# Quantising the residual stream in steps between the first attention's projection groups, with the last tiles through the score banks and no barrier ahead of the quantised stage

## The chip, the cores and the metric

The kernel runs on the 8 NeuronCores of one Trainium2 chip. Each core works on one sequence of its own (4096 rows of 1024 numbers); the cores share no data, and all run the same program. The metric is the device time in microseconds of the slowest core.

On a core, TensorE (PE) multiplies 128-wide tiles into PSUM, VectorE (DVE) and ScalarE (ACT) work on SBUF and PSUM, GpSimd (POOL) works on SBUF, and SyncE (SP) issues every DMA of this kernel from one queue. Each engine takes its instructions in the order of the program; semaphores connect the engines.

## The reference, cut to what matters

Two layers, each with an attention and a feed-forward part, both of the form `x = x + layernorm(part(layernorm(x)))`:

```python
# attention: 8 heads of 128, causal, no bias
xn  = x / l2norm(x) * sqrt(1024) * gamma
q, k, v = split(xn @ w_qkv.T);  out = softmax(q @ k.T / sqrt(128) + causal) @ v @ w_out.T
# layer 0's second part: product of integers, row scales of both sides
lhs_scale = max(|lhs|, axis=2) / 127          # lhs = layernorm(x)
q_lhs = round(lhs / lhs_scale);  q_rhs = round(rhs / rhs_scale)
acc = q_lhs @ q_rhs;             out = acc * lhs_scale * rhs_scale
# layer 1's second part: three blocks of two 1024 x 1024 linear layers with
# 4-bit weights plus a rank-32 term, a layernorm and gelu between the two
```

What matters here is the seam between layer 0's two parts: every row of `x`, once the attention's output is normalised and added, has to be centred, its absolute maximum taken, scaled and rounded to integers before the integer product.

## The kernel before, in words

The program is written out by hand as one list of steps, `p.add(engine, ...)`; each engine gets its own steps in the order in which they stand there, with waits on semaphores. `PE`, `DV`, `AC`, `GP` and `DMA` add a step to TensorE, VectorE, ScalarE, GpSimd and SP. A DVE step waits for the DVE step before it.

`emit_attn` is one attention. First come the projections to k, q and v for eight blocks of 512 rows (L638, L643). Then 576 *steps* follow, `steps[i] = (qt, h, pr)`: for each block of 512 queries `qt`, each head `h` and each pair `pr` of key tiles of 128 (2 qt + 2 pairs). Step i puts these instructions down, in this order:

- ACT: the exponential of the scores (L765), of which the scores (PE, L756) were put down two steps earlier, into one of two score banks `PS` of 1024 columns; for a pair on the diagonal a mask on POOL (L772).
- PE: the scores of step i+2, then the product of the probabilities with v (L782), and at every second step the row sums (L799) into one bank `RS`.
- At a head's end DVE splits the row sums in a high and a low part (L811, L812); two steps later PE adds the four partial sums (L817, L819) into the bank `MISC`; later ACT forms the reciprocal (L824, L826) and DVE the head's result `feat` (L827).
- When a block of queries is done, its output projection waits in `out_q`: eight *groups*, two halves of 512 columns for each of four row tiles of 128. `out_group` (L850) takes one into `MISC`, every `max(1, (2*qt+2)*H // 11)` steps of the next block. DVE takes statistics of it (L856) and copies it to SBUF (L857). Behind a tile's second half it forms the inverse root in eight column instructions (`rsqrt_eps`, L283 to L288) and updates the residual row tile in one of three buffers (L862), SP stores it to `xbuf` and loads the tile three further into the buffer.
- `quantise_rhs` (a generator) makes the integer weights of the next part, one piece every eight steps.

The last block's eight groups follow after the last step, one after the other through `MISC`. Then comes `p.barrier()`: every engine waits for all that was begun.

`emit_mid` is the quantised stage, on 32 row tiles in pairs, a software pipeline with one pair per turn. `P1` to `P3` load a tile, take statistics (L995), centre it on ACT (L998), take the absolute maximum (L1008), scale (L1021) and round it on ACT (L1023). `Q` transposes the integers on PE and copies them out of PSUM on ACT (L1034); `G` is the integer product (L1043, 32 matmuls a pair). `Y` rescales on DVE (L1051) and sums squares on ACT (L1054); `E1`, `E2` normalise (ACT, L1072) and add to the residual on POOL (L1075); `L1`, `L2` take the next layer's statistics (DVE, L1084 to L1097) and prepare its input (ACT, L1101), `T` transposes that into `xn`. POOL also scales the next layer's weights there, two pieces per turn (`cast_w`, L984).

After a second barrier layer 1's attention runs with the same code, and after a third the last part (`emit_f1`).

## Time and profile before

| | us |
|---|---|
| median of 3 runs | 3982.25 (3980.55 to 4304.46) |
| the profiled execution, its own time | 3971.3 |
| its span, slowest core (core 4) | 3969.8 |
| layer 0: projections | 0 to 477 |
| layer 0: attention steps | 477 to 1321 |
| layer 0: last four tiles' projection | 1321 to 1365 |
| quantised stage, first to last integer product | 1390 to 1703 |
| layer 1: projections | 1728 to 2150 |
| layer 1: attention steps and last tiles | 2160 to 3029 |
| last part | 3040 to 3970 |

Over the span PE is busy for 84%, ACT for 55%, DVE for 53% and POOL for 23%. The profiled execution stands 11 us under the median. The share of the span says little about a stage: PE is busy for 88% of the attention steps and for 55% of the quantised stage. The views used are the windows (busy time of each engine in a stretch), the timeline (instructions with their start, length and the idle time ahead of them) and the groups of instructions by line.

### The profile page before, as it was taken

Reading aid. Unit: us, or ns where it says so; the run is one execution under the profiler, and the core shown is the slowest. Engines: PE = TensorE matmul, PEld = TensorE weight load, DVE = VectorE, ACT = ScalarE, POOL = GpSimd, SP = SyncE. Lnnn points to the kernel's source line nnn. Section 1 sums busy time; section 2 is a strip of 40 time slices with the busy share of each in tenths; the row PEclk is TensorE's granted clock in tenths of the full one; section 3 lists DMA queues with packets and bytes.
Section 4 is the critical chain, followed back from the end, with each engine's and each line's share of the span. In section 5 each row is a group of like instructions: output and inputs, shape, how many; then the busy total and the mean of one; then the engine's idle time right before and its main releaser. Section 6 shows DMA issues by size and latency. Waiting matters only on the chain.

```text
span 3969.8 us, 45734 instructions; the slowest of 8 cores (3946.3 to 3969.8 us)
## 1 busy us (share of the span) xinstructions
PE 3316.4 (84%) x16736; PEld 1382.8 (35%) x16736; DVE 2089.5 (53%) x3897; ACT 2195.0 (55%) x2660; POOL 912.4 (23%) x868
## 2 busy tenths in 40 slices
PE   5999768989999555579997789999994789879997
PEld 2444323333333122233333333333331334334442
DVE  5666455443222488855555544333224656685547
ACT  2211146777888367743332567888891554635543
POOL 2333210001100033236663100000000231433333
PEclk9999879999999777789998899999997899989999
DMA  5111212132110254236655111111003210140004
GB/s 197 53 59 54 97 41 80 64 85 71 52 52 34 80 180 154 85 109 186 181 177 186 43 75 69 54 43 43 22 32 124 101 54 27 38 165 1 1 1 159
DMA packets 93472, 330.47 MB, mean 83 GB/s; under 512 B 12416, under 2 KB 16000, under 8 KB 88384
## 3 DMA queue, kind: packets, MB, share of 16 engines
q1 hardware_dynamic: 93248, 327.56, 24.5%
q8 instruction: 132, 2.16, 0.2%
q14 instruction: 92, 0.75, 0.1%
HBM read 228.94 MB, written 98.57 MB: 83 GB/s over the span
## 4 chain that ended last, share of the span: by engine, by line
PE 55%; DVE 22%; ACT 15%; DMA 3%; issue 2%; POOL 1%; SPq 0%; DVEq 0%; POOLq 0%; ACTq 0%
PE pp L756 9%; PE pp L638 8%; PE pp L782 8%; ACT s_probs L765 6%; PE pp L850 5%; PE pp L643 5%; PE pp L1314 4%; PE pp L1043 4%; PE pp L1269 4%; PE pp L799 3%; ACT f_yg L1301 2%; ACT s_rcp L826 1%; PE pp L622 1%; ACT s_rcp L824 1%; DVE f_r L1293 1%
## 5 line engine op out<-in xcount | busy, mean ns | idle before, releaser
L765 ACT ACTIVATE s_probs<-pp,s_negM 128x1024 bf16<-128x1024 f32 (+2 forms) x1152 | 1123.4, 1039 | 211.1 <-PE pp L756 207.6
L756 PE MATMUL pp<-s_q,s_kT 128*128 128x512 bf16 (+3 forms) x2304 | 664.8, 371 | 74.0 <-ACT s_probs L765 58.5
L782 PE MATMUL pp<-s_probs,s_v 128*128 128x512 bf16 (+3 forms) x2304 | 659.1, 368 | 16.3 <-POOL s_probs L772 14.9
L772 POOL TENSOR_SCALAR_AFFINE_SELECT s_probs<-s_probs 128x256 bf16<-128x256 bf16 x256 | 104.5, 408 | 1479.0 <-ACT s_probs L765 1462.5
L1269 PE MATMUL pp<-f_h,f_w 128*128 128x512 bf16 x1536 | 363.9, 386 | 3.4 <-ACT f_h L1244 3.4
L1279 POOL TENSOR_TENSOR f_sq<-f_yg 128x512 bf16<-128x512 bf16 x192 | 210.7, 1097 | 548.5 <-ACT f_yg L1274 495.1
L756 PEld LDWEIGHTS pp<-s_q,s_kT 128*128 128x128 bf16 x2304 | 189.0, 99 | 383.8 <-ACT s_probs L765 188.3
L782 PEld LDWEIGHTS pp<-s_probs,s_v 128*128 128x128 bf16 x2304 | 222.8, 99 | 265.6 <-POOL s_probs L772 30.4
L799 PE MATMUL pp<-s_probs,ones 128*32 128x512 bf16 (+4 forms) x2304 | 244.5, 380 | 80.2 <-DVE s_lo L812 80.1
L850 PE MATMUL pp<-s_wq,s_feat 128*128 128x512 bf16 x1024 | 259.0, 398 | 42.6 <-DVE s_y L857 31.0
L811 DVE CAST s_hi<-pp 128x512 bf16<-128x512 f32 x128 | 88.5, 692 | 389.6 <-PE pp L799 384.2
L1043 PE MATMUL pp<-m_w,m_qT 128*128 128x512 bf16 x512 | 147.7, 460 | 143.9 <-ACT m_qT L1034 137.4
L856 DVE BATCH_NORM_STATS2 s_bst<-pp 128x6 f32<-128x512 f32 x128 | 89.4, 699 | 325.4 <-PE pp L850 323.3
L649 ACT ACTIVATE s_kT<-pp 128x512 bf16<-128x512 f32 x128 | 76.3, 597 | 315.5 <-PE pp L638 315.1
L1314 PE MATMUL pp<-f_yg,f_w 128*128 128x512 bf16 x1024 | 231.4, 387 | 21.2 <-DVE f_h L1319 12.4
L827 DVE TENSOR_TENSOR s_feat<-pp,s_rcp 128x512 bf16<-128x512 f32 x128 | 88.5, 692 | 283.4 <-ACT s_rcp L826 280.7
L1274 ACT ACTIVATE f_yg<-pp,bc 128x512 bf16<-128x512 f32 x192 | 127.8, 679 | 161.8 <-PE pp L1269 161.3
L1269 PEld LDWEIGHTS pp<-f_h,f_w 128*128 128x128 bf16 x1536 | 151.9, 99 | 186.9 <-issue 13.4
L652 POOL TENSOR_TENSOR s_sq<-s_kT 128x512 bf16<-128x512 bf16 x128 | 136.4, 1065 | 253.5 <-ACT s_kT L649 239.4
L657 ACT ACTIVATE s_qst<-pp 128x512 bf16<-128x512 f32 x128 | 75.4, 595 | 203.3 <-PE pp L638 203.3
L824 ACT ACTIVATE s_rcp<-pp 128x512 f32<-128x512 f32 x128 | 76.5, 597 | 180.2 <-PE pp L819 176.5
L1301 ACT ACTIVATE f_yg<-f_u,lbcol,lgcol 128x512 bf16<-128x512 bf16 x192 | 148.7, 809 | 45.8 <-DVE f_u L1299 45.2
(179 smaller groups left out, 5053.1 us busy)
## 6 DMA issues: line engine op xcount, KB each, us to landing
s_x<-x SPq DMA_DIRECT2D x64, 512.0 KB, 3.7
xbuf<-s_x SPq DMA_DIRECT2D x64, 512.0 KB, 2.6
s_fqi<-qwT SPq DMA_DIRECT2D x48, 512.0 KB, 5.0
s_fsc<-scT SPq DMA_DIRECT2D x48, 512.0 KB
qspill<-s_qst SPq DMA_DIRECT2D x16, 1024.0 KB, 5.0
s_q<-qspill SPq DMA_DIRECT2D x16, 1024.0 KB, 5.4
m_x<-xbuf SPq DMA_DIRECT2D x32, 512.0 KB, 4.7
xbuf<-m_x SPq DMA_DIRECT2D x32, 512.0 KB, 2.7
```

The source lines that it names most:

```text
L638: fn = lambda e, b=b, fi=fi, o=o, wb=wb, xn=xn: e.matmul(pf[b], wb[:, fi, o * 128:(o + 1) * 128], xn[:, fi, :], start=(fi == 0), stop=(fi ...
L643: fn = lambda e, b=b, fi=fi, tt=tt, hf=hf, xn=xn: e.matmul(pf[b], xn[:, fi, tt * 128:(tt + 1) * 128], S.wv[:, fi, hf * 512:(hf + 1) * 512] ...
L756: s_tok[i] = PE(lambda e, kc=kc, q0=q0, c0=c0, b=b, h=h, qt=qt: e.matmul(PS[b][:, c0:c0 + 512 - q0], S.kT[:, h, kc * 128:(kc + 1) * 128], ...
L765: tok = AC(lambda e, b=b, w=w, sl=sl, h=h, qt=qt: e.activation(S.probs[:, sl, 0:w], PS[b][:, 0:w], AF.Exp, bias=S.negM[:, h, qt:qt + 1], s ...
L782: tok = PE(lambda e, kc=kc, q0=q0, c0=c0, sl=sl, h=h, po=po, first=first, last=last: e.matmul(po[:, q0:512], S.v[:, kc, h * 128:(h + 1) * ...
L799: tok = PE(lambda e, out=out, ones=ones, sl=sl, c0=c0, q0=q0, first=first, pr=pr, qt=qt: e.matmul(out, ones, S.probs[:, sl, c0:c0 + 512 - ...
L850: tok = PE(lambda e, fi=fi, tt=tt, hf=hf: e.matmul(MISC, S.feat[:, qt % 2, fi, tt * 128:(tt + 1) * 128], S.wo[:, fi, hf * 512:(hf + 1) * 5 ...
L1043: tok = PE(lambda e, j=j, hf=hf: e.matmul(M.ps2[i][:, hf * 512:(hf + 1) * 512], Z.qT[:, i, j, :], Z.w[:, j, hf * 512:(hf + 1) * 512], star ...
L1269: tok = PE(lambda e, j=j, oc=oc, b=b: e.matmul(pf[b], F.w[i][:, j, oc * 128:(oc + 1) * 128], F.h[hb][:, j, :], start=(j == 0), stop=(j == ...
L1279: sqt.append((k, GP(lambda e, oc=oc, k=k: e.tensor_mul(F.sq[:, k, :], F.yg[yb][:, oc, :], F.yg[yb][:, oc, :]), ev, S["sq_free"][k])))
L1301: g_ready[g] = S["u_free"][n] = AC(lambda e, oc=oc, n=n: e.activation(F.yg[yb][:, oc, :], F.u[:, n, :], AF.Gelu, bias=M.lbcol[:, blk, oc:o ...
L1314: tok = PE(lambda e, j=j, oc=oc, b=b: e.matmul(pf[b], F.w[i][:, j, oc * 128:(oc + 1) * 128], F.yg[yb][:, j, :], start=(j == 0), stop=(j == ...
```

## The change: what it does

- **Quantising in steps.** In layer 0 a residual tile, once updated, is quantised inside the attention. Its work is put in a list `later` with the step at which it is put down: statistics one step after the tile's second group, centring and absolute maximum three after (the centring overwrites the tile and waits for its store), scaling five after, and the rounding to integers (ACT, from the tile to `qb`) eight after, with a store to a new array `q1` in DRAM. The load of the tile three further now stands behind that rounding. `P1` to `P3` of the quantised stage are gone; it loads the integers instead, and has one turn less. The copy of the transposed integers out of PSUM moves from ACT to DVE.
- **Spacing.** Groups are put down every `(2*qt+2)*H // 9` steps, and only when the tile two before is through with its quantising (`may_start`). The weight quantiser starts at step 100 instead of 150 and works on halves. Both layers share the spacing; the quantising is layer 0's alone.
- **Last tiles.** In both layers the last block's tiles go through the two score banks, both halves of a tile in one bank of 1024 columns, and DVE reads the bank itself instead of a copy.
- **No barrier** ahead of the quantised stage: single waits take its place. Half of the integer weights are asked for during the last block.
- The high and low part of the row sums have one buffer each instead of two; unused tiles are gone from the memory plan.

```diff
@@ emit_attn
-        hi, lo = S.hi[:, k, :], S.lo[:, k, :]
-        DV(lambda e: e.tensor_copy(hi, RS), rs, hl_free[k], wo_ok)
+        hi, lo = S.hi[:], S.lo[:]
+        DV(lambda e: e.tensor_copy(hi, RS), rs, st["hl"], wo_ok)
...
+    def residual(t, src):
+
+        b = t % 3
+        DV(lambda e: e.bn_aggr(S.mv[:, 0, :], S.bst[:, 0, :, :]))
+        rsqrt_eps(DV, S.mv[:, 0, 1:2], S.y8[:, 0:1], S.t8[:, 0:1], S.t8[:, 1:2])
+        r = DV(lambda e: e.scalar_tensor_tensor(
+            S.x[:, b, :], src, S.y8[:, 0:1], S.x[:, b, :], ALU.mult, ALU.add), xb_in[t])
+        xb_free[b] = x_done[t] = DMA(x_dst[t * 128:(t + 1) * 128, :], S.x[:, b, :], f"so{b}", r)
+        if q1 is not None:
+            quantise(t)
+        elif t + 3 < NT:
+            load_xb(t + 3)
+        return r
...
+        def stats():
+            for hf in (0, 1):
+                DV(lambda e, hf=hf: e.bn_stats(S.pst[:, hf, :], xs[:, hf * 512:(hf + 1) * 512]))
+            DV(lambda e: e.bn_aggr(S.pmv[:, i, :], S.pst[:]))
+
+        def centre():
+            DV(lambda e: e.tensor_scalar(xs, xs, mean, None, ALU.subtract), x_done[t])
+            DV(lambda e: e.tensor_reduce(c[0], xs, AX.X, ALU.max, apply_absolute_value=True))
+
+        def scale():
+            rsqrt_eps(DV, var, c[1], c[2], c[3])
...
+            st["t", i] = DV(lambda e: e.tensor_scalar(xs, xs, c[6], MAGIC, ALU.mult, ALU.add))
+
+        def integers():
+            a = xb_free[b] = AC(lambda e: e.activation(S.qb[:], xs, AF.Copy, bias=-MAGIC),
+                                st["t", i], q_done.get(t - 1), wo_ok)
+            q_done[t] = DMA(q1[t], S.qb[:], "qb", a)
+            if t + 3 < NT:
+                load_xb(t + 3)
+
+        later.extend([(now + d, t, f) for d, f in ((1, stats), (3, centre), (5, scale),
+                                                    (8, integers))])
...
+    def last_tiles():
...
+        for tt in range(4):
+            t, P = qt * 4 + tt, M.ps2[tt % 2]
...
+                DV(lambda e, hf=hf, P=P: e.bn_stats(S.bst[:, 0, hf, :],
+                                                    P[:, hf * 512:(hf + 1) * 512]), tok)
+            s_free[tt % 2] = (residual(t, P[:]),)
+
+            now += 6
+            run_later(now - 4)
+        run_later(now + 9)
...
-        if i > 150 and i % 8 == 4:
+        if i > 100 and i % 8 == 4:
             next(more, None)
-        per = max(1, (2 * qt + 2) * H // 11)
-        if out_q and i >= next_out and st["misc"]:
+        run_later(i)
+        if out_q and i >= next_out and st["misc"] and may_start(*out_q[0]):
+            per = max(1, (2 * qt + 2) * H // 9)
             out_group(*out_q.pop(0))
-            next_out = i + per
+            next_out = (next_out if next_out > i - per else i) + per
...
@@ emit_mid
-        qT_tok[t] = F["trq"][i] = AC(lambda e: e.activation(Z.qT[:, i, :, :], TRQ[i], AF.Copy), tok,
+        if t + 4 < NT:
+            load_q(t + 4)
+        qT_tok[t] = F["trq"][i] = DV(lambda e: e.tensor_copy(Z.qT[:, i, :, :], TRQ[i]), tok,
                                      F["qT"][i])
...
@@ build_fused_program
-    emit_attn(p, M, S, io, 0, side=quantise_rhs)
-    p.barrier()
+    Z, w0 = MidMem(nc, S), []
+    hand = emit_attn(p, M, S, io, 0, side=quantise_rhs, q1=q1, ahead=lambda free: w0.append(
+        ask_weights(p, Z, io, 0, free, *[(n, p.c(n)) for n in ("rq", "rr")])))
```

DVE in layer 0, one of the last tiles that are projected between the steps, kernel before: from the root's last steps to the head ends that follow (the numbers behind the L are lines; `s_feat` is a head's result).

```order
L287 SCALAR_TENSOR_TENSOR s_t_115<-s_y_114,s_t_115 128x1 [waits ve]
L288 TENSOR_SCALAR s_y_114<-s_t_115,s_y_114 128x1 [waits ve]
L862 SCALAR_TENSOR_TENSOR s_x<-s_y,s_y_114,s_x 128x1024 [waits ve,sx0]
L827 TENSOR_TENSOR s_feat<-pp,s_rcp 128x512 [waits ve,ae]
L811 CAST s_hi<-pp 128x512 [waits ve,mm]
L812 TENSOR_TENSOR s_lo<-pp,s_hi 128x512 [waits ve]
```

The same place with the change: the update of a tile is L814, the statistics L835, the centring L839 with the maximum L840, and then the root.

```order
L814 SCALAR_TENSOR_TENSOR s_x<-s_y,s_y_58,s_x 128x1024 [waits ve,sx2]
L835 BN_STATS s_pst<-s_x 128x6 [waits ve] x2
L836 BN_AGGR s_pmv<-s_pst 128x2 [waits ve]
L839 TENSOR_SCALAR s_x<-s_x,s_pmv 128x1024 [waits ve,so2]
L840 TENSOR_REDUCE s_pc<-s_x 128x1 [waits ve]
L215 TENSOR_SCALAR s_pc<-s_pmv 128x1 [waits ve]
L216 TENSOR_SCALAR s_pc<-s_pc 128x1 [waits ve]
L219 SCALAR_TENSOR_TENSOR s_pc<-s_pc 128x1 [waits ve]
```

Behind these stand five more instructions of the root and the following, the end of a tile's work on DVE, with the next head's sums behind it:

```order
L844 TENSOR_TENSOR s_pc<-s_pc 128x1 [waits ve]
L845 TENSOR_SCALAR s_pc<-s_pc 128x1 [waits ve]
L846 RECIPROCAL s_pc<-s_pc 128x1 [waits ve]
L847 TENSOR_TENSOR s_pc<-s_pc 128x1 [waits ve]
L848 SCALAR_TENSOR_TENSOR s_eps<-s_pc 128x1 [waits ve]
L850 TENSOR_SCALAR s_x<-s_x,s_pc 128x1024 [waits ve]
L757 CAST s_hi<-pp 128x512 [waits ve,mm]
L758 TENSOR_TENSOR s_lo<-pp,s_hi 128x512 [waits ve]
```

Nineteen instructions came in between a tile's update and the next head's sums; the first of them that waits for anything but DVE waits for the tile's store (`so2`).

ACT in the same block, with the change: the exponentials (L711), a head's reciprocal (L770, L772) and the rounding to integers (L853).

```order
L711 ACTIVATE s_probs<-pp,s_negM 128x1024 [waits mm] x4
L770 ACTIVATE s_rcp<-pp 128x512 [waits mm]
L772 ACTIVATE s_rcp<-s_rcp 128x512 [waits ae]
L711 ACTIVATE s_probs<-pp,s_negM 128x1024 [waits mm] x2
L853 ACTIVATE s_qb<-s_x 128x1024 [waits ve,qb]
L711 ACTIVATE s_probs<-pp,s_negM 128x1024 [waits mm] x8
```

In the kernel before only exponentials and reciprocals stand there, and none of the exponentials waits for DVE. L853 is new, waits for DVE (`ve`), and has exponentials ahead and behind.

SP at the seam, with the change: the last tiles' stores (`xbuf`, `q`), and then the first loads of the quantised stage.

```order
L205 DMA xbuf<-s_x 128x1024 [waits ve]
L205 DMA q<-s_qb 128x1024 [waits ae] x2
L205 DMA m_w<-rq 128x4x1024 [waits mm]
L205 DMA m_q<-q 128x1024 [waits mm,qb]
L205 DMA m_q<-q 128x1024 [waits qb]
L205 DMA m_rs<-rrow 128x1024
L205 DMA m_x<-xbuf 128x1024 [waits so0]
```

In the kernel before the stores are followed by the barrier and four loads `m_x<-xbuf`; now the last two integer stores stand ahead of the stage's loads in SP's order.

## Rows read from the trace of the kernel before

**Rows 1.** Windows: stretch, its length, PE, PEld, DVE, ACT, POOL busy; PEclk, DMA.
```profile
477.00:1321.00 844.00, 745.46 (x4032) 287.52 (x4032) 333.66 (x642) 635.61 (x705) 72.55 (x144) 0.94 0.19 64
1321.00:1364.90 43.90, 23.07 (x64) 7.22 (x64) 23.65 (x57) 0.00 (x0) 0.00 (x0) 0.77 0.13 48
1390.00:1702.00 312.00, 171.76 (x958) 83.23 (x957) 252.17 (x552) 224.29 (x292) 97.67 (x54) 0.75 0.38 136
...
546.40:603.90 57.50, 50.09 (x268) 20.93 (x268) 38.78 (x79) 37.69 (x49) 6.53 (x16) 0.94 0.15 56
1156.40:1315.40 159.00, 151.99 (x846) 57.64 (x844) 41.40 (x83) 138.22 (x144) 8.75 (x18) 1.00 0.09 33
```
**Rows 2.** Timeline, last block of layer 0: start, length, engine, instruction, idle before.
```profile
1207.87 1.89 PE L850 MATMUL pp<-s_wq,s_feat 128*128 128x512 bf16 x8
...
1209.79 0.70 DVE L856 BATCH_NORM_STATS2 s_bst<-pp 128x6 f32<-128x512 f32 x1 [2.54 <-PE pp L850]
...
1210.23 1.11 ACT L765 ACTIVATE s_probs<-pp,s_negM 128x1024 bf16<-128x1024 f32 x1 [1.28 <-PE pp L756]
...
1211.50 0.15 DVE L283 TENSOR_SCALAR s_t<-s_mv 128x1 f32<-128x1 f32 x1
...
1211.53 5.44 ACT L765 ACTIVATE s_probs<-pp,s_negM 128x1024 bf16<-128x1024 f32 x5 [0.18 <-PE pp L756]
...
1213.45 1.28 DVE L862 SCALAR_TENSOR_TENSOR s_x<-s_y,s_y,s_x 128x1024 f32<-128x1024 f32 x1
...
1214.76 0.32 SPq L273 DMA_DIRECT2D xbuf<-s_x  x1
...
1217.66 0.33 SPq L273 DMA_DIRECT2D s_x<-x  x1
...
1217.76 0.38 PE L782 MATMUL pp<-s_probs,s_v 128*128 128x512 bf16 x1
```
**Rows 3.** Groups of DVE instructions by form: busy us, mean ns, idle before.
```profile
L995 DVE BATCH_NORM_STATS2 m_bst<-m_x 128x6 f32<-128x512 f32 x64 | 44.4, 694 | 10.6 <-DMA m_x<-xbuf 6.4
...
L1008 DVE TENSOR_REDUCE m_amax<-m_d 128x1 f32<-128x1024 f32 x32 | 39.0, 1220 | 3.7 <-DVE m_mv L1086 0.5
...
L1021 DVE TENSOR_SCALAR m_d<-m_d,m_inv 128x1024 f32<-128x1024 f32 x32 | 25.7, 802 | 1.1
```
**Rows 4.** Groups of ACT instructions by form, the integer copy of the quantised stage.
```profile
L1023 ACT ACTIVATE m_q<-m_d 128x1024 bf16<-128x1024 f32 x32 | 32.1, 1047 | 10.5 <-DVE m_d L1021 10.5
```
**Rows 5.** Timeline of PE, the quantised stage's first product and its last two.
```profile
1389.82 9.10 PE L1043 MATMUL pp<-m_w,m_qT 128*128 128x512 bf16 x32 [3.68 <-ACT m_qT L1034]
...
1676.16 9.29 PE L1043 MATMUL pp<-m_w,m_qT 128*128 128x512 bf16 x32 [9.41 <-ACT m_qT L1034]
...
1693.80 9.00 PE L1043 MATMUL pp<-m_w,m_qT 128*128 128x512 bf16 x32 [6.56 <-DVE m_mv L1086]
```
**Rows 6.** Timeline, the last pair of tiles of the quantised stage but one.
```profile
1686.88 1.06 ACT L1054 ACTIVATE m_junk<-m_y 128x1024 bf16<-128x1024 f32 x1 [1.77 <-DVE m_y L1051]
...
1690.37 2.37 ACT L1072 ACTIVATE m_y<-m_y,m_nb,m_r 128x1024 f32<-128x1024 f32 x2 [0.43 <-DVE m_nb L1069]
...
1691.69 4.83 POOL L1075 TENSOR_TENSOR m_x<-m_x,m_y 128x1024 f32<-128x1024 f32 x2 [12.81 <-ACT m_y L1072]
...
1692.07 1.42 DVE L1084 BATCH_NORM_STATS2 m_bs<-m_x 128x6 f32<-128x512 f32 x2
...
1695.07 1.47 DVE L1092 TENSOR_TENSOR m_l<-m_sv,m_sve 128x2 f32<-128x2 f32 x1
...
1697.37 2.38 ACT L1101 ACTIVATE s_prep<-m_x,m_nb,m_cf 128x1024 bf16<-128x1024 f32 x2 [2.53 <-DVE m_nb L1097]
```
**Rows 7.** Timeline of PE, the last tiles' projection in layer 0.
```profile
1321.27 3.57 PE L850 MATMUL pp<-s_wq,s_feat 128*128 128x512 bf16 x8 [2.50 <-DVE s_feat L827]
...
1331.12 1.90 PE L850 MATMUL pp<-s_wq,s_feat 128*128 128x512 bf16 x8 [1.52 <-DVE s_y L857]
...
1336.16 3.46 PE L850 MATMUL pp<-s_wq,s_feat 128*128 128x512 bf16 x8 [3.15 <-DVE s_y L857]
```

More of the change, by code:

```diff
@@ L858, in out_group @@
         if hf == 1:
[L859 to L865 removed]
+            y_free[ys] = residual(t, S.y[:, ys, :])
@@ new lines, in emit_attn @@
+    x_done, q_done, later = {}, {}, []
+    def residual(t, src):
[10 more added lines that the diff above has]
+        return r
@@ L866, in out_group, with run_later, may_start @@
             if t + 3 < NT:
                 load_xb(t + 3)
+        later.extend([(now + d, t, f) for d, f in ((1, stats), (3, centre), (5, scale),
+                                                    (8, integers))])
+        later.sort(key=lambda v: v[0])
+    def run_later(upto):
+        while later and later[0][0] <= upto:
+            later.pop(0)[2]()
+    def may_start(qt, n):
+        t = qt * 4 + n // 2
+        return t in xb_in and all(v[1] > t - 2 for v in later)
+    def last_tiles():
+        nonlocal now
+        qt = NQ - 1
+        for tt in range(4):
+            t, P = qt * 4 + tt, M.ps2[tt % 2]
+            for hf in (0, 1):
+                for fi in range(NF):
+                    tok = PE(lambda e, fi=fi, tt=tt, hf=hf, P=P: e.matmul(
+                        P[:, hf * 512:(hf + 1) * 512], S.feat[:, qt % 2, fi, tt * 128:(tt + 1) * 128],
+                        S.wo[:, fi, hf * 512:(hf + 1) * 512], start=(fi == 0), stop=(fi == NF - 1),
+                        skip_group_check=True),
+                        *((st["feat", qt], *s_free[tt % 2], wo_ok) if fi == 0 else ()),
+                        inc=(fi == NF - 1))
+                DV(lambda e, hf=hf, P=P: e.bn_stats(S.bst[:, 0, hf, :],
[4 more added lines that the diff above has]
+        run_later(now + 9)
@@ L875, in emit_attn @@
     out_q = []
-    next_out = 0
+    next_out = now = 0
     for i in range(N):
         qt, h, pr = steps[i]
+        now = i
         ready[i] = emit_exp(i)
@@ L894, in emit_attn @@
             todo.sort(key=lambda x: x[0])
-        if i > 150 and i % 8 == 4:
+        if i > 100 and i % 8 == 4:
             next(more, None)
-        per = max(1, (2 * qt + 2) * H // 11)
-        if out_q and i >= next_out and st["misc"]:
+        if ahead and qt == NQ - 1 and h == 6 and pr == 0:
+            for _ in more:
+                pass
+            ahead(last_S[qt - 1])
+        run_later(i)
+        if out_q and i >= next_out and st["misc"] and may_start(*out_q[0]):
+            per = max(1, (2 * qt + 2) * H // 9)
+            assert out_q[0][0] == qt - 1
             out_group(*out_q.pop(0))
-            next_out = i + per
+            next_out = (next_out if next_out > i - per else i) + per
     for _, f in todo:
         f()
-    for n in range(8):
-        out_group(NQ - 1, n)
+    assert not out_q
+    run_later(now + 9)
+    last_tiles()
+    ends = [(n, p.c(n)) for n in ("mm", "ve", "ae", "qb", "rq") if p.c(n)]
+    return {"S": last_S[NQ - 1], "AV": av, "x": x_done, "q": q_done, "xb": xb_free, "all": ends,
+            "ps": [s_free[0][0], s_free[1][0]], "po": po_free, "rs": st["rs"], "misc": st["misc"]}
 class MidMem:
@@ L1126, in emit_mid @@
     nw = 0
-    for n in range(NB + 3):
-        e, g, l = n - 2, n - 1, n - 3
+    for g in range(NB + 2):
+        e, l = g - 1, g - 2
         if 0 <= e < NB:
             E1(e)
-        if n < NB:
-            P1(n)
+        if g < NB:
+            Q(2 * g)
+            Q(2 * g + 1)
         if 0 <= e < NB:
             E2(e)
-        if 0 <= g < NB:
-            Q(2 * g)
-            Q(2 * g + 1)
+        if g < NB:
             G(2 * g)
```

222 lines of the change are left out of this document (74 added, 148 removed).

## The prediction

> **What bounds the kernel now.** I read the stages first (windows), then one projection block inside the attention instruction by instruction (timeline), then the quantised stage.
>
> The attention of layer 0 takes 844 us and PE is busy for 745 of them at a granted clock of 0.94: it is PE's stage [rows 1]. In its last block of 512 queries (159.0 us for 128 steps, 1.24 us a step) PE is busy for 152.0 us and ACT for 138.2 [rows 1]. ACT has little room there: between two projection groups its exponentials run without a gap, five in 5.44 us [rows 2]. DVE has room: 41.4 of 159.0 us, and 38.8 of 57.5 in the first block that projects [rows 1].
>
> The quantised stage is nobody's at full speed: 312 us with DVE busy for 252, ACT 224, PE 172 at clock 0.75 [rows 1]. Its 16 products of a pair of tiles begin between 1389.82 and 1693.80, 15 periods of 20.3 us [rows 5]. DVE with some 16 us a period, and the waits between DVE and ACT, set it.
>
> The last four tiles' projection of layer 0 is a chain too: 43.9 us, PE 23.1 and DVE 23.7 of them, one after the other [rows 1].
>
> **What the change costs in layer 0's attention.** 28 tiles are quantised between the steps, four per block from the second block on. Per tile DVE gets: two statistics of 0.69 and their aggregate (0.2), 1.7 us with gaps; centring 0.80 and absolute maximum 1.22, 2.1 us; an inverse root of eight column instructions (1.95 us, from the first of them to the update behind them), five more column instructions of 0.15 to 0.2 and the scaling of 0.80, 3.8 us [rows 2, 3]. Together 7.6 us, or 213 us on an engine with 510 us idle. The busy time is covered; the order is not.
>
> The last step of a tile is on ACT, which takes its instructions in order: the integer copy is put eight steps behind the tile's last projection group, between exponentials, and waits for DVE's scaling. So I compare two arrival times, from the end of that group, T = 1207.87 + 1.89 = 1209.76 [rows 2].
> - DVE: the residual update ends at 1214.73 (T+5.0). The centring overwrites the tile, so it waits until the tile is stored; the next load into that buffer, which waited for the same store, was issued at 1217.66 (T+7.9) [rows 2]. The statistics fit ahead of that. Then 2.1 + 3.8: T+13.8.
> - ACT: the exponential of step +3 starts at 1210.23, those of +4 to +8 end at 1216.97 (T+7.2) [rows 2].
>
> ACT therefore stands still for 6.6 us, and all exponentials queue behind it. It then needs 1.05 us for the copy [rows 4]. PE's next probability product is 0.8 us behind its exponential (1217.76 against 1216.97) [rows 2], so PE loses 6.6 + 1.05 - 0.8 = 6.9 us per tile. Neither engine can win that back: PE was busy 96% of this block.
> - Last four blocks, 16 tiles: 16 x 6.9 = 110 us.
> - Blocks three and four, 8 tiles: a step lies between 1.80 (57.5 / 32) and 1.24 us [rows 1], near 1.5, so ACT comes about 1.6 us later: 5 us each, 40 us.
> - Block two, 4 tiles in 32 steps: here DVE fills up. Per tile 7.6 + 5.0 + 1.4 (the first half's group), per head some 2.1 us for sums and division: 56 + 17 = 73 us, with waits for stores 77, against 57.5. That is +20 by DVE's work and +40 if each tile waits; I take 30.
> - After a standstill PE restarts at its lower clock. In the last projection eight products took 3.46 us behind 3.15 us of idleness and 1.90 us behind 1.52 us [rows 7]: 1.6 us, 28 times, 45 us.
>
> Sum +225 us. Lower end: only ACT's own copies, 28 x 1.05 = 29 us (work is added, so no gain); upper end 28 x (6.9 + 1.7) = 241, with 1.7 us as the cold start of the quantised stage (32 products in 9.29 us behind a long pause against 32 x 1.90 / 8 = 7.6) [rows 5, 7].
>
> What else queues behind these waits: on DVE, behind the centring, a head's sums, for which PE's next row sums wait; they fall inside the same standstill. On SP the load of tile t+3 moves from behind the store (T+7.9) to behind the integer store (T+15); it is needed three tiles later, 30 steps and more, except in block two, where my 30 us hold it.
>
> The longer spacing of the groups (divisor 9 for 11) moves no work; at best both attentions gain evenly spread groups. Bounds 0 and -14 us (a microsecond a block), I take -5, for layer 1. One buffer for the high and low part of the sums costs nothing: the one before was read two steps after the head's end, and heads are four steps or more apart from the second block on; in the first, the division already stands between them on DVE. The halved loads of the weight quantiser add eight small DMAs and eight reductions beside idle DVE: nothing.
>
> **The last tiles.** Without the copies out of PSUM and with two banks, DVE's own chain is left: two statistics, aggregate, root and update, 5.0 us a tile [rows 2]. In layer 1: a first group of 3.6 us [rows 7], its other half 3.3, then 4.3 + 3 x 5.0: 26 us instead of 43.9, **-18 us**. In layer 0 the four tiles carry the 7.6 us as well: 6.2 + 4 x 12.6, the integer copy at +57. SP is in order too: the stage's first loads stand behind the last tile's integer store. With some 6 us for loads, transposes and the copy out of PSUM the first product starts at +64.5 instead of +68.5 (1321.27 to 1389.82 [rows 5, 7]): **-4 us**. Dropping the barrier overlaps almost nothing.
>
> **The quantised stage** loses the statistics, maximum and scaling on DVE (some 8 us a pair), two ACT passes over each tile (a third moves to DVE, 0.7 us each), and one turn of the pipeline. What closes the loop is read from a turn in which that first part is already absent [rows 6], with its zero at the end of the product before (1676.16 + 9.29 = 1685.45) [rows 5]: square sums done at +2.6; normalising on ACT from +4.9 to +7.3; POOL's two additions to +11.1; the column product L1092 starts at +9.6 and ends with them (1696.54 and 1696.52); preparation on ACT +11.9 to +14.3; the next pair's square sums 2.3 us later, +16.6. The period is 16.6 - 2.6 = **14.0 us**. PE, whose next product now waits only for DVE's copies (+3.9), would end at +13.2 even with the 9.29 us of a cold start [rows 5]. POOL's first weight cast waits for the end of all attention work and for its load behind ten tiles' loads, with the first additions behind it; they are due two periods later, which covers it. 15 x (20.3 - 14.0) = **-94 us**. Ends: 12.0 us if L1092 did not wait (-124), 17.3 us, the period of the very turn I read from (1702.80 - 1685.45; -45).
>
> L1092, two columns, took 1.47 us where a column instruction takes 0.15; the row statistics ahead of it (two in 1.42 us) ran undisturbed beside the same additions [rows 2, 6]. The Trainium skill, SBUF — State Buffer, Who interferes with whom, gives the rule: a VectorE instruction with two SBUF inputs and a GpSimd instruction that reads SBUF exclude one another for a whole instruction. By that rule the weight casts on POOL hold up the next two-input column product too, in the 11 periods that have casts, and the gain would be some 12 us smaller.
>
> **Sum**: 225 - 5 - 18 - 4 - 94 = +104 on an execution of 3971.3 us (span 3969.8). The median of the runs, 3982.25, stands 11 us above it: 3982 + 104 = **4086 us**.
>
> **Rivals.**
> - *The wait at ACT is absorbed* (18%): if PE's and ACT's leads let the copy slip behind later work, only 29 us are paid: 3982 + 29 - 121 = 3890, faster by 2.3%. It decides at a DVE chain below some 8 us. For it: DVE idles three quarters of the last block. Against: the store alone lands at T+7.9.
> - *Half of it* (15%): where the next group falls within the eight steps, ACT comes 2 to 4 us later, and slower steps do the same. 112 us instead of 225: 3973, no change.
> - *The stage keeps 17.3 us a pair* (10%), because another wait (two loads, two stores and two integer tiles per pair on one in-order queue) takes the place of the removed ones: 4086 + 49 = 4135.
> - *A table load at each integer copy* would cost ACT far more, but copies and scalings stand between exponentials' and roots' work everywhere without one; no chance given.
>
> **How the numbers follow.** The forecast has 57% and a range of its own of 4000 to 4150 (attention +150 to +241, the stage -60 to -110). About 2% of 3982, 80 us, is what a measurement of this kernel tells from no change: the line is at 4062. Of the forecast's 57% I put 38 above it and 19 below. With the third rival slower has 48%; same gets 19 + 15 + 5 (a part of the first rival, which lies close to the other line, 3902) = 39%, faster 13%. The range leaves out most of the first rival and the far end of the third: 3960 to 4165.
>
> **What would show it.** Right: ACT idle 5 us or more ahead of the integer copy, released by DVE's scaling, 24 times; layer 0's attention above 1000 us with layer 1's near 825; products of the quantised stage 14 us apart; the last projection of layer 1 near 26 us. Wrong: the copy released at once, or both attentions equally long; then the first rival holds. A period above 17 us speaks for the third.

## The result and the profile after

The changed kernel is slower: ratio of its runs to those of the kernel before **1.0274, 95% interval [1.0245, 1.0304]**. The profiled execution took 4087.57 us (span 4086.0, core 5), where 4086 was forecast. The median of its four runs, 4146.32 us, holds two in which some cores ran at a lower granted clock, and the ratio leaves such runs out.

Cut into stages at the same instructions in both traces, median of the eight cores, in us:

| stage | before | after | difference | forecast |
|---|---|---|---|---|
| up to layer 0's first exponential | 476.8 | 473.8 | -3.0 | |
| layer 0's attention, first to last exponential | 834.8 | 1021.7 | **+186.9** | +225 |
| from there to the first integer product | 70.7 | 71.4 | +0.7 | -4 |
| integer products, first to last matmul | 312.4 | 230.1 | **-82.3** | -94 (-82 by the rule) |
| from there to layer 1's first projection | 25.4 | 31.7 | +6.3 | |
| layer 1's projections | 435.1 | 440.4 | +5.3 | |
| layer 1's attention | 819.0 | 830.2 | +11.2 | -5 |
| layer 1's last tiles and the last part | 990.5 | 973.3 | -17.2 | -18 |
| sum | 3964.7 | 4072.6 | +107.9 | +104 |

So the sum was right within 4 us, while its largest term was off by 38 and several others by 5 to 16. Windows of layer 0's attention before, and of the kernel after: layer 0's attention, its second and its last block of queries, and layer 1's attention (columns as in [rows 1], then the rate of the DMA in GB/s).

```profile
479.40:1315.40 836.00, 742.43 (x4018) 286.64 (x4018) 331.70 (x639) 633.11 (x703) 72.14 (x143) 0.95 0.19 64
```

```profile
479.80:1504.90 1025.10, 797.18 (x4018) 298.19 (x4018) 523.57 (x1180) 664.56 (x730) 76.53 (x143) 0.87 0.19 60
546.00:635.00 89.00, 60.65 (x272) 22.45 (x272) 68.35 (x158) 42.21 (x54) 6.50 (x16) 0.79 0.16 51
1314.80:1504.90 190.10, 161.86 (x847) 59.64 (x844) 68.96 (x160) 142.59 (x148) 10.82 (x19) 0.92 0.12 41
2283.20:3112.60 829.40, 743.73 (x4018) 286.60 (x4018) 320.92 (x628) 633.99 (x702) 56.25 (x127) 0.95 0.14 52
```

Compare layer 0's attention with the line before and with layer 1's: the same 4018 matmuls, but now they are busy for 797 us instead of 742 (744 in layer 1) at a granted clock of 0.87 instead of 0.95, and PE stands still for 228 us instead of 94 (86). No engine is full: in the last block DVE is busy for 69 of 190 us (41 of 159 before [rows 1]). In the second block it comes closest, with 68 of 89.

What ended those standstills is in the waits of PE in layer 0's attention (waited for; us in total, times, longest), first before, then after, and below them ACT's wait at the integer copy:

```profile
PE pp L799 <- DVE s_lo L812: 40.6, 12, 19.6
PE pp L756 <- ACT s_probs L765: 29.4, 38, 2.4
PE pp L782 <- POOL s_probs L772: 14.5, 2, 13.6
```

```profile
PE pp L745 <- DVE s_lo L758: 100.4, 19, 17.7
PE pp L702 <- ACT s_probs L711: 93.5, 40, 9.3
PE pp L763 <- DVE s_y L803: 13.9, 7, 4.8
PE pp L728 <- DVE s_feat L773: 13.6, 4, 6.2
...
ACT s_qb L853 <- DVE s_x L850: 111.4, 26, 8.5
```

The forecast knew of one of these, exponentials behind the copy: they grew by 64 us. Another, a head's row sums that wait until DVE has split the sums of the head before, grew by 60. The timeline shows both. One tile of the last block, from its last projection group on:

```profile
1423.47 1.90 PE L796 MATMUL pp<-s_wq,s_feat 128*128 128x512 bf16 x8
...
1429.06 1.44 DVE L814 SCALAR_TENSOR_TENSOR s_x<-s_y,s_y,s_x 128x1024 f32<-128x1024 f32 x1
...
1429.84 2.12 ACT L711 ACTIVATE s_probs<-pp,s_negM 128x1024 bf16<-128x1024 f32 x2 [0.42 <-PE pp L702]
...
1433.74 0.75 DVE L839 TENSOR_SCALAR s_x<-s_x,s_pmv 128x1024 f32<-128x1024 f32 x1 [1.54 <-DMA xbuf<-s_x]
...
1438.64 0.76 DVE L850 TENSOR_SCALAR s_x<-s_x,s_pc 128x1024 f32<-128x1024 f32 x1
1439.49 1.06 ACT L853 ACTIVATE s_qb<-s_x 128x1024 bf16<-128x1024 f32 x1 [7.53 <-DVE s_x L850]
1439.50 0.69 DVE L757 CAST s_hi<-pp 128x512 bf16<-128x512 f32 x1
...
1440.97 0.62 PE L745 MATMUL pp<-s_probs,ones 128*32 128x512 bf16 x4 [7.66 <-DVE s_lo L758]
```

This is the forecast step by step: the group ends at T = 1423.47 + 1.90 = 1425.37; DVE is through at T+14.0 (T+13.8 forecast); ACT ends its exponentials at T+6.6 (T+7.2) and stands for 7.5 us (6.6). But the split L757 stands behind the scaling too, so that PE would have waited until 1440.97 for it even if ACT had gone on. Another tile, 39 us earlier, where the head ends sooner:

```profile
1384.73 0.39 PE L745 MATMUL pp<-s_probs,ones 128*32 128x512 bf16 x4
...
1387.09 1.28 DVE L814 SCALAR_TENSOR_TENSOR s_x<-s_y,s_y,s_x 128x1024 f32<-128x1024 f32 x1
...
1388.41 1.42 DVE L835 BATCH_NORM_STATS2 s_pst<-s_x 128x6 f32<-128x512 f32 x2
...
1390.18 0.69 DVE L757 CAST s_hi<-pp 128x512 bf16<-128x512 f32 x1
1390.90 0.69 DVE L758 TENSOR_TENSOR s_lo<-pp,s_hi 128x512 bf16<-128x512 f32 x1
...
1391.65 0.62 PE L745 MATMUL pp<-s_probs,ones 128*32 128x512 bf16 x4 [4.57 <-DVE s_lo L758]
...
1397.45 1.06 ACT L853 ACTIVATE s_qb<-s_x 128x1024 bf16<-128x1024 f32 x1 [0.50 <-DVE s_x L850]
```

Here the sums were ready at 1385.1, and update and statistics stood ahead of their split. PE stood for 4.57 us, ACT with it, and so ACT came late enough to find its integers nearly scaled. In ACT's timeline 13 of the 28 copies in steps have 5 us or more of idleness ahead of them, where 24 were forecast: at ten of the other eleven the sums had held up PE just before, for 3.5 to 6 us, by the same queue on DVE, and ACT had lost its lead to that.

In the quantised stage the product starts every 14.9 us while POOL has weights to scale, ten periods in a row, and every 14.2, 14.2 and 13.9 us behind them (20.3 before); the first two periods are 11.8 and 18.6 us long. The piece that closes the turn, with such weights on POOL and, 74 us later, without:

```profile
1701.35 2.34 POOL L1086 TENSOR_TENSOR m_x<-m_x,m_y 128x1024 f32<-128x1024 f32 x1 [0.20 <-ACT m_sve L1099]
1701.42 2.29 DVE L1103 TENSOR_TENSOR m_l<-m_sv,m_sve 128x2 f32<-128x2 f32 x1
1703.74 0.17 DVE L1104 TENSOR_SCALAR m_l<-m_l 128x2 f32<-128x2 f32 x1
1703.86 1.12 POOL L1029 TENSOR_SCALAR s_wv<-s_x,gcol 128x1024 bf16<-128x1024 f32 x1 [0.17 <-POOL m_x L1086]
...
1704.14 0.84 DVE L1106 SCALAR_TENSOR_TENSOR m_cf<-m_l,m_sve 128x2 f32<-128x2 f32 x1
...
1775.19 2.29 DVE L1103 TENSOR_TENSOR m_l<-m_sv,m_sve 128x2 f32<-128x2 f32 x1
...
1777.91 0.16 DVE L1106 SCALAR_TENSOR_TENSOR m_cf<-m_l,m_sve 128x2 f32<-128x2 f32 x1
```

L1106 takes 0.84 us beside the scaling of a weight (L1029) and 0.16 without: 0.68 us, the difference between 14.9 and 14.2.

### The profile page after: what moved, and what is told of

It reads as the page before. It is cut to its first block, busy times and chain, and to the rows that moved or that the text cites. A ratio compares the mean times of both kernels' runs of the same rounds, so it can differ in the third digit from the quotient of the medians.

```text
span 4086.0 us, 46166 instructions; the slowest of 8 cores (4057.0 to 4086.0 us)
## 1 busy us (share of the span) xinstructions
PE 3361.2 (82%) x16736; PEld 1398.5 (34%) x16736; DVE 2202.5 (54%) x4279; ACT 2132.8 (52%) x2580; POOL 919.8 (23%) x868
## 4 chain that ended last, share of the span: by engine, by line
PE 48%; DVE 29%; ACT 12%; DMA 6%; issue 3%; POOL 1%; SPq 1%; DVEq 0%; POOLq 0%; ACTq 0%
PE pp L702 8%; PE pp L728 7%; PE pp L585 7%; PE pp L590 5%; PE pp L796 4%; PE pp L1324 4%; ACT s_probs L711 4%; PE pp L1279 4%; PE pp L745 3%; DMA s_fsc<-scT 2%; DVE s_x L814 2%; ACT f_yg L1311 2%; DMA xbuf<-s_x 1%; DVE f_r L1303 1%; PE pp L569 1%
## 5 line engine op out<-in xcount | busy, mean ns | idle before, releaser
L711 ACT ACTIVATE s_probs<-pp,s_negM 128x1024 bf16<-128x1024 f32 (+2 forms) x1152 | 1128.9, 1039 | 228.2 <-PE pp L702 224.3
L702 PE MATMUL pp<-s_q,s_kT 128*128 128x512 bf16 (+3 forms) x2304 | 689.0, 383 | 135.1 <-ACT s_probs L711 121.5
L728 PE MATMUL pp<-s_probs,s_v 128*128 128x512 bf16 (+3 forms) x2304 | 682.8, 380 | 18.3 <-DVE s_feat L773 14.3
L718 POOL TENSOR_SCALAR_AFFINE_SELECT s_probs<-s_probs 128x256 bf16<-128x256 bf16 x256 | 113.2, 442 | 1658.3 <-ACT s_probs L711 1643.6
L802 DVE BATCH_NORM_STATS2 s_bst<-pp 128x6 f32<-128x512 f32 x112 | 78.2, 699 | 335.6 <-PE pp L796 333.6
L757 DVE CAST s_hi<-pp 128x512 bf16<-128x512 f32 x128 | 88.5, 691 | 298.2 <-PE pp L745 290.8
L796 PE MATMUL pp<-s_wq,s_feat 128*128 128x512 bf16 x896 | 217.2, 386 | 11.4 <-DVE s_feat L773 6.5
L745 PEld LDWEIGHTS pp<-s_probs,ones 128*32 128x32 bf16 (+1 forms) x2304 | 66.1, 94 | 375.7 <-issue 184.4
L770 ACT ACTIVATE s_rcp<-pp 128x512 f32<-128x512 f32 x128 | 76.4, 597 | 219.1 <-PE pp L765 209.4
```

What stands on the lines that cost most here:

```text
L702: s_tok[i] = PE(lambda e, kc=kc, q0=q0, c0=c0, b=b, h=h, qt=qt: e.matmul(PS[b][:, c0:c0 + 512 - q0], S.kT[:, h, kc * 128:(kc + 1) * 128], ...
L711: tok = AC(lambda e, b=b, w=w, sl=sl, h=h, qt=qt: e.activation(S.probs[:, sl, 0:w], PS[b][:, 0:w], AF.Exp, bias=S.negM[:, h, qt:qt + 1], s ...
L728: tok = PE(lambda e, kc=kc, q0=q0, c0=c0, sl=sl, h=h, po=po, first=first, last=last: e.matmul(po[:, q0:512], S.v[:, kc, h * 128:(h + 1) * ...
L745: tok = PE(lambda e, out=out, ones=ones, sl=sl, c0=c0, q0=q0, first=first, pr=pr, qt=qt: e.matmul(out, ones, S.probs[:, sl, c0:c0 + 512 - ...
L796: tok = PE(lambda e, fi=fi, tt=tt, hf=hf: e.matmul(MISC, S.feat[:, qt % 2, fi, tt * 128:(tt + 1) * 128], S.wo[:, fi, hf * 512:(hf + 1) * 5 ...
```

## The experiments

The theory is that layer 0's loss comes from the order of the work, in which two queues hold PE up, ACT's behind the integer copy and DVE's ahead of the split of the sums, and that no engine has too much work, but for the second block. Its rivals are one of the two queues alone, or the added work itself.

**The copy later.**

```diff
-        later.extend([(now + d, t, f) for d, f in ((1, stats), (3, centre), (5, scale),
-                                                    (8, integers))])
+        late = 8 if t < 4 else 14
+        later.extend([(now + d, t, f) for d, f in ((1, stats), (3, centre), (5, scale),
+                                                    (late, integers))])
```

> One edit: from the third block of queries on, the integer copy on ACT stands 14 steps behind the tile's last projection group instead of 8, so that DVE's scaling is done when ACT comes. In the changed kernel's attention of layer 0 (1025 us, 189 more than before) PE waited 93.5 us for exponentials (29.4 before) and 100.4 us for a head's sums on DVE (40.6 before). Theory (two separate queues: ACT behind the copy, DVE's in-order work ahead of the sums): the wait for exponentials falls back to about 30 us and with it a part of the slow-clock time, the wait for sums stays near 100 us; attention of layer 0 at 940 to 965 us, the run at 4000 to 4025. Rival (one standstill that both waits share, since the sums stand behind the same DVE work): the wait for sums takes over what ACT gives up; attention above 1000 us, the run at 4060 or more.

The result lies between theory and rival. Layer 0's attention took 982.5 us (median of the cores, as in all that follows), 39 less than in the changed kernel; the profiled run took 4044.13 us. PE's waits in the attention:

```profile
PE pp L745 <- DVE s_lo L758: 128.2, 27, 18.4
PE pp L702 <- ACT s_probs L711: 28.2, 29, 2.4
```

ACT's wait at the copies in the steps fell from 111.4 to 1.0 us and PE's wait for exponentials to 28, as the theory had it. But the wait for sums did not stay at 100: it took over 28 of the 65 us that the exponentials gave up. Part of the standstill was shared.

**DVE's work in another order.**

```diff
         if hf == 1:
-            y_free[ys] = residual(t, S.y[:, ys, :])
+            def finish():
+                y_free[ys] = residual(t, S.y[:, ys, :])
+            steps_of = {1: (0, 1, 2, 2, 3), 2: (1, 1, 4, 1, 3)}.get(qt + 1, (2, 2, 6, 2, 3))
+            gap[t] = steps_of
...
     def run_later(upto):
         while later and later[0][0] <= upto:
+            if upto < N:
+                qt, h, pr = steps[upto]
+                if qt >= 2 and 1 <= 2 * qt + 1 - pr <= 2:
+                    return
             later.pop(0)[2]()
...
     def may_start(qt, n):
+        q, _, pr = steps[now]
+        if q >= 3 and not 3 <= pr <= 2 * q - 2:
+            return False
```

The five numbers are the gaps, in steps, ahead of update, statistics, centring, scaling and integer copy.

> The same work in another order, from the third block on (and in layer 1's attention for the residual update): the residual update, statistics, centring, scaling and integer copy of a tile are issued one after the other with gaps of 2, 2, 6, 2 and 3 steps behind the tile's last group (shorter ones in the third block, the old order in the second), none in the two steps ahead of a head's end, and no projection group there either or in the first steps of a head. No instruction is added or taken away. Theory (the loss is order, not work): PE's wait for sums falls from 100 to below 45 us (17.7 of them are the first one at the start of the attention), the wait for exponentials to about 30; layer 0's attention at 865 to 895 us, layer 1's at 805 to 820 instead of 830; the run at 3905 to 3950. Rival (DVE's or ACT's added work itself costs PE its lead, wherever it stands): layer 0's attention stays above 950 us, the run above 4000.

The ratio to the kernel before is 0.991 [0.9891, 0.993]: 0.9% below it, where the changed kernel was 2.7% above. Layer 0's attention took 917.6 us, more than the 865 to 895 expected, but below the rival's 950; layer 1's took 788.2, 31 below the kernel before and better than expected. PE's waits in layer 0's attention:

```profile
PE pp L702 <- ACT s_probs L711: 80.8, 44, 8.4
PE pp L745 <- DVE s_lo L758: 23.0, 6, 18.0
```

The sums are cleared, exponentials are not: scaling and copy had only three steps between them, and ACT stood 60.6 us ahead of 24 copies, about 2.2 us at eleven of them.

**Both.** The same, with `(1, 1, 4, 1, 5)` in the third block and `(2, 2, 6, 2, 6)` behind it.

> As e2_dve_order, with the integer copy three steps later (6 behind the scaling instead of 3; 5 in the third block). In e2_dve_order ACT still stood 60.6 us ahead of the copies, some 2.2 us at most of them, and PE waited 80.8 us for exponentials (29.4 before), while its wait for sums had gone to 23.0 us, 18.0 of them the first one. Theory (both queues had to be cleared, ACT's and DVE's): ACT's wait at the copies below 10 us outside the second block, PE's wait for exponentials near 30 us, layer 0's attention at 862 to 885 us against 914 to 918; the run 35 to 55 us below e2_dve_order, 3885 to 3905. Rival (the remaining 80 us over before are DVE's and ACT's work, not the wait): the attention stays above 900 us.

This is better than expected: the ratio is **0.9752 [0.9733, 0.9771]**, and layer 0's attention takes 850.8 us, 171 less than in the changed kernel with the same instructions. PE's waits:

```profile
PE pp L702 <- ACT s_probs L711: 40.4, 40, 5.5
PE pp L745 <- DVE s_lo L758: 23.5, 6, 19.5
```

At the start of the fifth block one copy still has 5.0 us of idleness ahead of it, behind that none. So the order was the larger part of the loss. What the added work costs in this order is seen beside layer 1, which has the same order without the quantising; the lines are from e7_both below, the third and fourth block and then the last two, layer 0 ahead of layer 1:

```profile
633.90:808.30 174.40, 151.98 (x832) 59.21 (x832) 132.74 (x302) 130.99 (x152) 13.14 (x32) 0.97 0.22 78
2215.40:2367.90 152.50, 147.20 (x830) 58.10 (x829) 86.72 (x176) 124.94 (x146) 13.33 (x32) 1.00 0.21 78
1035.10:1329.50 294.40, 287.59 (x1596) 108.47 (x1594) 139.24 (x323) 265.31 (x281) 26.94 (x41) 1.00 0.18 60
2587.40:2877.50 290.10, 286.68 (x1598) 109.11 (x1596) 80.57 (x160) 259.28 (x272) 14.34 (x32) 1.00 0.09 33
```

In the last two blocks the quantising of eight tiles costs 4 us, although DVE does 59 us more there: where it does not stand in the way, the work costs next to nothing. In the third and fourth block it still costs 22 us; no run shows whether another order would win them back. The later copy is worth 39 us in the old order and 67 in the new one, since as long as one of the queues holds PE up it takes over from the other.

**The second block** takes 88 to 89 us in all of these kernels against 57.5 [rows 1]; its order of work is the old one in all of them. The kernel for this experiment is e7_both, below, and it leaves out most of the block's quantising.

```diff
+        if t < 4:
+            st["t", i] = r_tok
+            DV(lambda e: e.memset(S.eps[:, t:t + 1], 1e-5))
+            later.append((now + 8, t, integers))
+            later.sort(key=lambda v: v[0])
+            return
...
```

> e7_both, with the statistics, centring, maximum and scaling on VectorE left out for the four tiles that are quantised in the second block of queries; the integer copy and its store stay. The second block took 66.9 and 57.5 us for the first two blocks before, and 88 to 90 for the second in every kernel with the change, whatever its order elsewhere; VectorE was busy for 68.1 of 88.1 us there, and PE waited for features and copies behind it. Theory (VectorE's queue is the second block's limit: 4 x 7.6 us of work in 32 steps): without it the block takes 60 to 66 us, and layer 0's attention 822 to 830 instead of 851. Rival (the narrower spacing of its groups, or ACT's copies, cost the block): it stays above 80 us.

```profile
546.80:611.60 64.80, 52.71 (x267) 20.69 (x272) 41.52 (x85) 41.26 (x53) 6.54 (x16) 0.92 0.19 69
```

The block took 64.8 us and the attention 825.6, 23.6 less: the theory held. With 27 of the 68 us of DVE work go 23 us of the block: here the amount of work counts, which is more than the 57.5 us that the whole block took before. The edit also takes away the wait for the tile's store, but that was 2.0 us in e2_dve_order's second block. Of the 7 us that are left the spacing has the larger part: layer 1's second block, with the spacing and without copies, took 62.5 us against 57.9 before.

**The column products of the quantised stage.**

```diff
-        DV(lambda e: e.tensor_mul(Z.l2[:], Z.sv[:], Z.sve[:]))
+        for i in (0, 1):
+            DV(lambda e, i=i: e.tensor_scalar(Z.l2[:, i:i + 1], Z.sv[:, i:i + 1], Z.sve[:, i:i + 1],
+                                              None, ALU.mult))
...
```

> One edit in the quantised stage: the column products that read two tiles in one VectorE instruction (sv x sve, then the coefficient and the offset, 2 columns each) are written as per-column instructions with one tile and one column as scalar, six for three. In the changed kernel the first of them took 2.29 us beside POOL's additions and the second 0.84 us beside POOL's weight cast, 0.16 us each without POOL at work; a pair of tiles took 14.9 us with casts and 14.2 without. Theory (a two-input VectorE instruction waits for POOL's, and this wait stands in the loop that closes the period): both waits go, the period falls to 12.2 to 12.8 us with and without casts, the stage to about 190 us from 221, the run by some 30 us. Rival (the period is closed by something else, the products on PE or ACT's order, and the wait is cover): the period stays within 0.5 us of 14.9 and 14.2.

The theory fell in this form: the stage took 230.3 us from first to last matmul (230.1 in the changed kernel; the 221 above runs to the last product's start), behind the first two its periods were 14.4 to 14.8, and the ratio was 1.0296 [1.0271, 1.032]. The timeline shows why:

```profile
1694.83 2.34 POOL L1086 TENSOR_TENSOR m_x<-m_x,m_y 128x1024 f32<-128x1024 f32 x1 [0.20 <-ACT m_sve L1099]
1694.90 0.46 DVE L1104 TENSOR_SCALAR m_l<-m_sv,m_sve 128x1 f32<-128x1 f32 x2
1695.39 1.80 DVE L1106 TENSOR_SCALAR m_l<-m_l 128x2 f32<-128x2 f32 x1
```

The products ran beside the addition. The next instruction, one input of two columns and two numbers, was held until the addition's end (1697.17). So it is written per column as well:

```diff
-        rdy["l1"] = DV(lambda e: e.tensor_scalar(Z.l2[:], Z.l2[:], 32.0, 1e-12, ALU.mult, ALU.max))
+        for i in (0, 1):
+            rdy["l1"] = DV(lambda e, i=i: e.tensor_scalar(
+                Z.l2[:, i:i + 1], Z.l2[:, i:i + 1], 32.0, 1e-12, ALU.mult, ALU.max))
```

> As e3_columns_one_input, and the next instruction too (times 32, at least 1e-12) per column. In e3_columns_one_input the two per-column products ran undisturbed beside POOL's addition (0.46 us for two), but the next instruction, one input of 128x2 with two numbers as scalars, took 1.80 us and ended with POOL's addition; the period stayed 14.6. Theory (what POOL holds up is not only an instruction with two inputs, but also a one-input form over two columns): over one column it runs undisturbed, nothing of the chain is left to hold up, and the period falls to 12.6 to 13.4 us; the stage to some 200 us from 230. Rival (whatever VectorE instruction comes first behind the two products waits for POOL; or the turn is closed elsewhere): the period stays at 14.2 to 14.9 us.

```profile
1702.95 2.34 POOL L1086 TENSOR_TENSOR m_x<-m_x,m_y 128x1024 f32<-128x1024 f32 x1 [0.20 <-ACT m_sve L1099]
1703.03 0.46 DVE L1104 TENSOR_SCALAR m_l<-m_sv,m_sve 128x1 f32<-128x1 f32 x2
1703.53 0.34 DVE L1107 TENSOR_SCALAR m_l<-m_l 128x1 f32<-128x1 f32 x2
1703.90 0.17 DVE L1109 RECIPROCAL m_l<-m_l 128x2 f32<-128x2 f32 x1
```

Nothing in this chain is held any more. Behind the first two periods, which stay at 13 and 20 us, the period is 13.2 us (13.5 twice) with weights and without, and the stage takes 211.2 us: 19 less, where some 30 had been expected. The run has no ratio of its own; e7_both repeats the 211.2 us. So the wait stood in the loop, and the form of the instruction decides whether it is held.

**All of it in one kernel.**

> e5_order_and_later and e6_all_columns_single in one kernel. If both theories hold, layer 0's attention is 862 to 885 us, layer 1's 786 to 790, the quantised stage some 200 us from first to last product group, and the run at 3850 to 3880, 2.5 to 3% below the kernel before. If the stage's period doesn't move, 3885 to 3905; if the attention stays at e2_dve_order's, 3905 to 3935.

The ratio to the kernel before is **0.9733 [0.965, 0.9816]**, and the profiled run took 3855.66 us. The interval is too wide to set the kernel apart from e5_order_and_later; that both edits add up is read from the stages: layer 0's attention 849.2 us, layer 1's 788.2, the quantised stage 211.2. Its two attentions:

```profile
478.00:1329.50 851.50, 751.12 (x4018) 287.45 (x4018) 523.85 (x1180) 658.15 (x731) 76.12 (x143) 0.93 0.22 72
2089.20:2877.50 788.30, 730.65 (x4018) 284.18 (x4018) 320.96 (x628) 634.02 (x703) 56.91 (x127) 0.97 0.15 55
```

In layer 0 DVE does the same 524 us of work as in the changed kernel; PE is busy 46 us less for the same matmuls, at a granted clock of 0.93 instead of 0.87.

**Layer 1's attention, +11 us.** One number was changed, `H // (9 if q1 is not None else 11)`:

> One number: in layer 1's attention the projection groups are spaced by the old divisor 11 instead of 9; layer 0 keeps 9. The changed kernel's attention of layer 1 took 827.8 to 831.9 us over the eight cores, against 816.8 to 820.7 before, where -5 had been forecast. Theory (the spacing puts more groups ahead of a head's end, so that the sums wait more: 46.3 against 39.5 us): layer 1's attention falls back to 816 to 822 us. Rival (the single buffer of the sums' high and low part, or the tile's update taken as one piece of DVE work, costs it): it stays at 828 to 832 us.

Layer 1's attention took 922 to 926 us over the cores, which fits neither; the next expectation, for the same kernel, says why this decides nothing.

> The kernel of e4_divisor_11 again, which ran with all eight cores at a granted clock of 0.77 to 0.78 and so can't be set beside the others (layer 1's attention 922 to 926 us). Theory (spacing 9 puts more groups ahead of a head's end): at the usual clock layer 1's attention takes 816 to 822 us, against 828 to 832 with 9. Rival (the single buffer of the sums' parts): 828 to 832 us.

It took 825.8 us, 822.4 to 828.5 over the cores, between theory and rival. The spacing is worth some 4 of the 11 us (with spacing 9 the same code took 830.8 us in e1 and 829.6 in e3). The waits for sums, which the theory made responsible, fell only from 46.3 to 44.3 us on the slowest cores. Then the second buffers came back, in layer 1 alone:

```diff
+        two = q1 is None
+        hi, lo = (S.hi2[:], S.lo2[:]) if two and k else (S.hi[:], S.lo[:])
...
```

> e8_divisor_11 with two buffers for the high and low part of the sums in layer 1 again, as before the change. Layer 1's attention took 816.8 to 820.7 us over the cores before, 827.8 to 831.9 with the change and 822.4 to 828.5 with the old divisor. Theory (the single buffer holds the next head's split until the sum products have read it): 817 to 821 us. Rival (the buffers cost nothing; the residue is the order of the residual update and the load behind it): 822 to 828 us.

It took 825.3 us, 823.3 to 829.0: the single buffer costs nothing. What makes up the other 6 us is open; the order of e2_dve_order takes 42 us off the same attention.

## Why the prediction was right, and where it was not

- **Layer 0's attention, +225 against +187.** The arrival times at the copy were right (T+14.0 and T+6.6 against 13.8 and 7.2), and so was the second block (+31.5 against +30). The failed step is "ACT therefore stands still for 6.6 us", counted for every tile: it happened at 13, 12 of the 16 tiles in the last four blocks and one of the 8 in the third and fourth, while at most others the sums had stopped PE before, for 3.5 to 6 us. "They fall inside the same standstill" was true only of sums that end behind the copy's place; the sums are a queue of their own, as the first two experiments showed. So the third and fourth block cost 18.5 and 20.2 us, 39 where 53 had been put down with their restarts.
- **The last four blocks, 136 with their restarts against 120.** Most of these 16 us are a term that the forecast had at nothing, the change of the weight quantiser. Before, PE stood 13.6 us in layer 0's sixth block until POOL had masked a tile (L772), the third line of the waits before. POOL's queue shows why:

```profile
869.52 0.95 POOL L772 TENSOR_SCALAR_AFFINE_SELECT s_probs<-s_probs 128x256 bf16<-128x256 bf16 x2 [10.34 <-ACT s_probs L765]
893.36 1.26 POOL L316 TENSOR_TENSOR s_rb<-s_rb,s_ri 128x512 f32<-128x512 f32 x1 [22.89 <-DMA s_rb<-rhs]
894.76 0.94 POOL L772 TENSOR_SCALAR_AFFINE_SELECT s_probs<-s_probs 128x256 bf16<-128x256 bf16 x2
```

The quantiser's first product (L316) waited for its loads, and the mask stood behind it: the same fault of order, in the kernel before. Seven of its eight cores lost 8 to 14 us at that place; in the changed kernel PE waits for masks 2.2 us in all. Whether the earlier start or the halves took it away, no run shows. By layer 1's sixth block, which had no such wait, the last four would have cost some 135 us; that this is the forecast's 136 is partly luck, since four of their 16 standstills had another cause than the one it counted.
- **Restarts at the low clock, 45.** PE is busy 55 us longer for the same matmuls: the term was right in kind and somewhat small.
- **Spacing, -5 against +11.** It was wrong in sign. "Moves no work" was true, but e8_divisor_11 gives 4 of the 11 us to the spacing; the rest is open, and not the buffers, as e10_two_sum_buffers showed.
- **Layer 1's last tiles, -18 against -17.2.** From the first group to the end of the last update 24.7 us (26 forecast), one update every 5.1 us (5.0).
- **Layer 0's last tiles and the barrier, -4 against +0.7.** From the second on the updates end every 12.6 us, as forecast; the first product starts 66.0 us behind the first group, where 64.5 had been worked out. The 68.5 us that it was set against are those of the slowest core alone: on the others the first product stood 63.6 to 66.4 us behind the first group before, so there was nothing to gain.
- **The stage, -94 against -82.** The period is 14.9 with weights and 14.2 without, for 14.0. The total is that of the version by the rule of the Trainium skill (SBUF — State Buffer, Who interferes with whom): 12 us less in the periods with casts. The trace agrees with the rule, 0.84 against 0.16 us for L1106, but ten such waits make 7 of the 12 us; the rest is shared by the first two periods, 30.4 us together, and by 14.2 for 14.0, so that the total fits so well is luck. The same section of the Trainium skill says that `tensor_scalar`, too, can enter a mode that takes the port shared with GpSimd; e3 and e6 agree, with 1.80 us over two columns and 0.17 over one.
- **Not forecast:** 6.3 us behind the last product and 5.3 in layer 1's projections (432 to 447 us over the cores, 433 to 438 before). No experiment looked for their cause; the same code for the projections took 434 to 439 us in the other kernels, so part of the 5.3 is spread between runs.
- **The rivals.** The wait was not absorbed: ACT stood for 111 us ahead of the copies. The second rival, ACT late by some microseconds, did happen at the tiles where the sums had stopped PE first; but what ACT was spared there PE had already lost. The stage did not keep 17.3 us a pair, and no table load stands between the steps.

The sum came out so close by cancelling: the attention had 38 us too many, and the spacing (16), the stage (12), layer 0's last tiles (5) and the two stages not forecast (12) had too few. That 4086 and 4087.57 lie still closer is luck once more: the forecast added its 104 us to a median of three runs, 11 us above the execution that the stages are read from. In the attention PE's standstills grew by 134 us where 180 had been put down at one place: 64 of them stood there, 60 at the sums. The mechanism forecast was half of what happens.

## What to carry to other kernels

When work is slipped between the steps of a pipeline on in-order engines, work out for every engine when each dependent instruction arrives and what is queued behind it, on the engine that does the new work as well as on the one that takes over its result. Cut the new work into pieces, put none of it ahead of what the bottleneck is about to ask for, and leave the hand-over to another engine late: here that turned +2.7% into -2.5% with the same instructions. Where the work itself exceeds the time (68 us of DVE work in a block that took 57.5), no order can give all of it back; how far another order would help the second block was not tried.

## What the hardware showed that was not expected

- A VectorE instruction with one input of 128x2 and two numbers took 1.80 us beside a POOL addition and ended with it; the same over 128x1 took 0.17 us beside the same addition, and products with a column as scalar 0.23 us each. Statistics of 128x512 (0.71 us each) ran undisturbed, too.
- A standstill of some 7 us cost PE more than its length. This had been forecast, and the traces add the clock: in the stretch behind the 7.66 us that ended at 1440.97, here as a window, the changed kernel's granted clock was at 0.50, the lower of its two levels.

```profile
1440.97:1445.20 4.23, 4.23 (x13) 1.45 (x14) 0.69 (x1) 3.86 (x6) 0.00 (x0) 0.50 0.81 246
```

Over layer 0's attention the same 4018 matmuls were busy for 797 us at a granted clock of 0.87, in e7_both for 751 at 0.93; in e7_both's last two blocks, where no wait of PE was longer than 1 us, the clock stayed at 1.00.
